# Another order of the attention work on ScalarE and VectorE

## What is computed

```python
xn = _layernorm(x, axis=-1)
q_latent, kv_latent = xn @ wq_down, xn @ wkv_down        # 192 and 64 wide
q = concat([q_latent @ wq_nope, rope(q_latent @ wq_rope)])
k = concat([kv_latent @ wk_nope, rope(kv_latent @ wk_rope)])
scores = einsum('bthd,bshd->bhts', q, k) / 192 ** 0.5     # causal mask
out = einsum('bhts,bshd->bthd', softmax(scores), kv_latent @ wv_up) @ wo
x = x + out + experts(xn)        # 32 experts, the best 8 of each token
```

## Time and profile before

| | before |
|---|---|
| median of 3 runs | 1176.25 us (1175.97 to 1178.59) |
| the profiled execution | 1180.77 us, its span 1179.0 us |
| TensorE busy | 1115.1 us, 95% of the span |
| VectorE busy | 723.4 us, 61% |
| ScalarE busy | 636.7 us, 54% |
| GpSimd busy | 493.7 us, 42% |

### The profile page before, as it was taken

How to read it: one execution, slowest core, us unless ns; L and a number is a source line. 1 busy time by engine, 2 the same in 40 slices (tenths; PEclk the granted TensorE clock), 3 DMA queues, 4 the chain that set the end, 5 groups by cost and what they waited for, 6 DMA issues and landing times. The chain is left out here.

```text
span 1179.0 us, 22440 instructions
## 1 busy us (share of the span) xinstructions
PE 1115.1 (95%) x7360; PEld 911.2 (77%) x7360; DVE 723.4 (61%) x1554; ACT 636.7 (54%) x1285; POOL 493.7 (42%) x386
## 2 busy tenths in 40 slices
PE   5859999999999999999999999899999999999997
PEld 3547778788788787787887887777888887888886
DVE  6657776676776776776776675545444445444444
ACT  3446666666666666666666666534343333334342
POOL 1083644643653653663653653222333332333332
PEclk9979999999999999999999999989999999999999
DMA  6101001001001001001000010065433333533332
GB/s 232 36 1 36 2 1 36 1 1 34 0 0 35 0 0 34 0 0 35 0 3 14 0 60 15 19 192 166 123 105 114 110 108 96 158 107 111 114 105 97
DMA packets 26309, 67.85 MB, mean 58 GB/s; under 512 B 3028, under 2 KB 9428, under 8 KB 26264
## 3 DMA queue, kind: packets, MB, share of 16 engines
q1 hardware_dynamic: 26120, 67.24, 18.8%
q10 hardware_dynamic: 144, 0.07, 0.0%
HBM read 62.82 MB, written 4.47 MB: 57 GB/s over the span
## 5 line engine op out<-in xcount | busy, mean ns | idle before, releaser
L736 ACT ACTIVATE prob<-ps_s,nm 128x128 f32<-128x128 f32 (+7 forms) x256 | 189.4, 740 | 209.0 <-DVE nm L896 208.1
L1339 POOL TENSOR_TENSOR hl<-hf,hh 128x512 fp32r<-128x512 f32 x96 | 123.6, 1287 | 295.4 <-ACT hh L1276 295.4
L896 DVE CUSTOM_DVE_ANT_0 ps_s<-ps_s,causal 128x128 f32<-128x128 f32 (+7 forms) x256 | 195.3, 765 | 54.4 <-PE ps_s L554 46.3
L565 PE MATMUL ps_t<-ident,prob 128*128 128x128 f32 x1152 | 177.2, 276 | 8.2 <-ACT pt L746 4.9
L565 PEld LDWEIGHTS ps_t<-ident,prob 128*128 128x128 f32 x1152 | 135.7, 141 | 36.1 <-issue 16.4
L577 PE MATMUL ps_o<-pt,kvn 128*64 128x128 f32 x2304 | 154.0, 278 | 0.5 <-DVE pt L905 0.4
L577 PEld LDWEIGHTS ps_o<-pt,kvn 128*64 128x64 f32 x2304 | 123.2, 136 | 33.3 <-issue 25.0
L905 DVE COPY pt<-ps_t 128x128 f32<-128x128 f32 (+2 forms) x192 | 102.1, 532 | 52.6 <-PE ps_t L565 52.2
L1308 DVE TENSOR_TENSOR gs<-gs,routing 128x512 f32<-128x512 f32 x64 | 44.3, 692 | 137.8 <-ACT gs L1272 137.8
L1276 ACT ACTIVATE hh<-hf 128x512 fp32r<-128x512 f32 x96 | 60.7, 633 | 121.6 <-DVE hf L1313 121.6
L1272 ACT ACTIVATE gs<-ps_g 128x512 f32<-128x512 f32 x96 | 57.4, 598 | 121.4 <-PE ps_g L1231 121.4
(11 more groups left out here) (271 smaller groups left out, 2571.4 us busy)
## 6 DMA issues: line engine op xcount, KB each, us to landing
routing<-wT_scratch SPq DMA_DIRECT2D x34, 256.0 KB, 3.7
raw_a<-in_e SPq DMA_DIRECT2D x17, 384.0 KB, 3.1
cosv<-in_e SPq DMA_DIRECT2D x17, 384.0 KB, 3.1
sinv<-wT_scratch SPq DMA_DIRECT2D x17, 384.0 KB, 3.6
raw<-in_e SPq DMA_DIRECT2D x17, 384.0 KB, 3.0
routing<-wT_scratch SPq DMA_DIRECT2D x16, 384.0 KB, 3.2
raw_a<-in_a SPq DMA_DIRECT2D x8, 512.0 KB, 3.3
raw_b<-in_b SPq DMA_DIRECT2D x8, 480.0 KB, 3.9
```

What stands on the lines that cost most here:

```text
L565: mm = nc.tensor.transpose(ps_t[x][:, at * P:(at + 1) * P], prob[t % 2][e][:, j * P:(j + 1) * P], ident[:, :])
L736: nc.scalar.activation(prob[t % 2][e][:, 0:len(halves) * width].rearrange("p (h k) -> p h k", k=width), ps_s[e][:, 0:len(halves), 0:width] ...
L896: nc.vector.tensor_tensor_reduce(out=s_ps, in0=s_ps, in1=bias, scale=-1.0, scalar=-MASKED, op0=ALU.add, op1=ALU.min, accum_out=nm[:, e:e + ...
L1339: nc.gpsimd.tensor_tensor(hl[:, c, :], hf[:, c, :], hh[:, c, :].bitcast(F32), ALU.subtract).then_inc(h_lo, 1)
```

## The change

Nothing is added or taken out; instructions of ScalarE and VectorE change places.

- ScalarE, tile 6: `latent_hi` of `QL1` now stands ahead of the first exponent, and `out_hi` behind the second `take_turned` (it stood ahead of the first exponent).
- ScalarE: `rope_hi` of `QR0` and of `KR0` stand at the end of tiles 3 and 4 (before: 4 and 5). `rope_hi` of `KR1` stands at the end of tile 0 (before: 1).
- VectorE, tile 2: `rope_products` of `KR0` stands behind the first maximum (before: ahead of it).
- VectorE, tile 3: `latent_low` of `QL0` stands behind the first maximum (before: ahead of it).

```diff
--- before.py
+++ after.py
@@ ScalarE, body(i), loop over the tiles t @@
-                        if t == TPC + 2:
-                            out_hi(s, 0, misc(i, b, "Yp1") if earlier else None)
+                        if more and t == TPC + 2:
+                            latent_hi(i, b, 1, 1 - b)
                         exponent(s, t, 0)
...
                         if more and t == 2:
                             latent_hi(i, b, 0, 1 - b)
-                        if more and t == TPC + 2:
-                            latent_hi(i, b, 1, 1 - b)
                         if has and (t == 0 or t > TPC):
                             take_turned(sp, tp, 1, 0)
+                        if t == TPC + 2:
+                            out_hi(s, 0, misc(i, b, "Yp1") if earlier else None)
                         exponent(s, t, 1)
                         if t == 0 and earlier:
                             widen(s - 1, 1)
-                        if more and t in (TPC, TPC + 1):
-                            rope_hi(s + 1, 0, 1 - b, (t - TPC,))
-                        if earlier and t == 1 and more:
+                        if more and t in (TPC - 1, TPC):
+                            rope_hi(s + 1, 0, 1 - b, (t - TPC + 1,))
+                        if earlier and t == 0 and more:
                             rope_hi(s, 1, b, (1,))
@@ VectorE, body(i), loop over the tiles t @@
                         if more and t == 1:
                             rope_products(i, b, "QR0", s + 1)
-                        if more and t == 2:
-                            rope_products(i, b, "KR0", s + 1)
-                        if more and t == 3:
-                            latent_low(i, b, 0, s + 1, 1 - b)
...
                         maximum(s, t, 0)
...
+                        if more and t == 2:
+                            rope_products(i, b, "KR0", s + 1)
                         if more and t == 3:
+                            latent_low(i, b, 0, s + 1, 1 - b)
                             rope_products(i, b, "QR1", s + 1)
```

## The result

The changed kernel took 1158.79 us, the median of 4 runs (1157.15 to 1159.53); the kernel before took 1176.20 (1175.97 to 1178.59). The ratio is 0.9845, with a 95% interval of 0.9828 to 0.9863: 1.5% faster. The forecast was 1153.5. So the time lies inside the stated range of 1151 to 1162, but 5.3 us above the forecast and 1.8 above the forecast's own range of 1151 to 1157: about a quarter of the expected 22.8 us is missing.

What follows compares the result with a forecast made beforehand. TensorE, busy 95% of the span, was taken as the bound, so only its waits counted: 8.0 + 6.0 + 6.8 + 1.1 + 0.9 = 22.8 us off 1176.25 gives 1153.5 us; own range 1151 to 1157, 8-in-10 range 1151 to 1162.

Steps and rivals of the forecast that it cites:

- A: In 14 of 16 stages tile 3's first scores wait for tile 2's first exponent; removing it gains 14 x 0.57 us.
- B: In six b = 0 stages the fold WA waits for `latent_low` of QL1; removing it gains 6 x 1.0 us.
- C: Between tiles 6 and 7 of b = 1 stages, turns wait for ScalarE's and VectorE's copies: 6 x 1.14 plus 1.1 us.
- D: A single TensorE wait at the start of the last stage; removing it gains 0.9 us.
- Covers at no cost: ScalarE's moved splits fit idle time before the exponents of tiles 1 and 4, so moving them costs zero.
- rival 2: The wait before tile 3's first scores moves to tile 5 in 14 stages: 8.0 us back, 1161.5 us; chance 0.10.
- Rival 3: Other waits end right behind the removed ones, so TensorE stands as long as before: 1176 us; chance 0.04.
- Rival 4: KR0's lows on GpSimd come too late for the next stage's first scores: slower, 1188 us; chance 0.06.
- The lock: VectorE instructions with two SBUF inputs and GpSimd instructions reading SBUF exclude each other; up to 0.78 us per blocked instruction.
- first rival: GpSimd blocks L881 or L883, delaying tile 7's maximum and exponent in 7 stages: 4.2 us back, 1157.7 us; chance 0.15.

Runs made afterwards that it cites:

- x5: The kernel before with VectorE's two moves alone (KR0's rotation, `latent_low` of QL0): 1176.63 us, ratio 0.9985 to 1.0004.
- x6: The kernel before with the `rope_hi` moves alone (QR0, KR0 and KR1): 1161.32 us, ratio 0.9835 to 0.9868.
- x9: The kernel before with only `rope_hi` of QR0 and KR0 moved, to the end of tiles 3 and 4: 1166.24 us (one run).
- x4: The kernel before with the tile-6 edit alone (`latent_hi` of QL1 and `out_hi` moved): 1167.26 us, ratio 0.9894 to 0.9927.
- x3: The changed kernel without its tile-6 edit (`latent_hi` of QL1 and `out_hi` as before): 1156.94 us, ratio 0.9803 to 0.9836.
- x2: The kernel before with L881 and L883 moved to the end of tile 4, while GpSimd makes its sums: 1188.47 us (one run).
- x1: The changed kernel with L881 and L883 moved ahead of the first maximum of tile 6, when GpSimd is idle: 1151.85 us.
- the repeat: The changed kernel measured again without any edit, beside other kernels on the same chip: 1157.14 us.
- x7: The changed kernel with `out_hi` of tile 6 put back ahead of the exponent and of QL1's splits: 1153.95 us, ratio 0.9791 to 0.9828.

## Why the prediction was right, and where it was not

**A, 14 x 0.57 = 8.0: right, with both its parts.** The exponent was late by KR1's splits, and the rotation of KR0 would have been the next to hold it, as the prediction worked out ("unmoved it would hold the exponent until 384.3"). x5 and x6 show one each: the first is the cause, the second the cause behind it. A place cost 0.61 and not 0.57; the earlier trace rows was a step with a score pass of another size.

**B, 6 x 1.0, and C, 6 x 1.14 + 1.1: the size right, the cause only half.** B was rounded down to 1.0 for nothing; it costs 1.14. C costs 1.13. But the prediction let them fall by two things at once, QL1's splits ahead of the exponent and an empty end of tile 5, and booked both under the tile-6 edit. Either is enough in the loop: x9 removes C and two thirds of B, x4 removes both. Only pair 0's C needs the tile-6 edit: x3 and x9 still have it, with printed waits of 0.52 and 0.49 us for ScalarE's copy and 0.19 for VectorE's (before 0.52 and 0.19). Two cures of one wait don't add: x4 gains 1.19 a loop, x3 3.18, together 4.37, and the change 2.85.

**D, 0.9: right.** No wait is printed at the start of the last stage.

**Covers at no cost: right.** The idle time ahead of tile 1's exponent fell from 1.96 to 0.80 us, and held KR1's 1.3; "some 0.6 left" was the forecast. Tile 5 didn't take over A (rival 2), but for the one place in pair 0, where 0.81 us of it stand. That stage lacks work of a stage before, and the prediction read its slack in a stage in the middle. Rival 3 is out, as the loop is 2.85 us shorter. Rival 4 is out: no wait for `keys` or `klo` came up at the start of a stage; x2, the one kernel that is slower than before, is so mainly by its waits for `yacc`.

**The lock: the step that failed.** The sum of the forecast put the lock at nothing, against its own first rival. That rival had the mechanism, the lines (L881, L883) and nearly the price: 4.2 us, where the loop and pair 0 give 6 x 0.71 + 0.45 = 4.7. It got a chance of 0.15 and came in all seven stages; the forecast, at 0.65, did not come. That the time is inside the stated range is due to this rival, which the range took in. Three of its steps fell short. First, whether the meeting happens was left as certain "in order, if not in time", and could have been worked out from rows of the kernel before:

```profile
362.13 2.63 POOL L1066 TENSOR_TENSOR klo<-t,khi 64x512 fp32r<-64x512 f32 x2 [0.22 <-ACT qhi L765]
366.51 0.35 DVE L881 CAST rhi<-raw_a 128x384 fp32r<-128x384 f32 x1
```

KR0's lows end at 364.76, and L881 starts 1.75 us later. By the prediction's own working the lows come 1.7 later, and `latent_low`, which stands ahead of `split_a` on VectorE, earlier. The two sides were moved towards each other until they met. Second, a blocked instruction cost more than 0.78: L881 1361 - 350 = 1.01 and L883 1526 - 558 = 0.97, together 1.98 against 1.6. Third, the reason against it, that the exponent of tile 7 is needed only in the next stage, looked at the exponent alone. What came late was the copy that stands behind it and QR1's two splits on ScalarE. So 1.98 us held up cost 0.71 by a path that the rival didn't have; that its price came so near is in part luck.

**The sum.** A pair of stages takes 2.85 us less, where 3.3 were forecast, and 3.56 less without the lock (x1). With the lock away (x1) the attention is 25.1 us shorter than before's, and the median 24.4: 22.8 was slightly too small. With it, 19.5 in the profiled executions. The medians say 17.4, and 19.1 for the repeat. The profile of before was 4.5 above its median; most of it is outside the attention, since it starts 1.7 us later there (70.84) and its end part is 2.3 us longer (409.9) than in most of the other kernels' profiles (69.03 to 69.4, and 407.6 to 408.6). So its waits can be taken for those of a median execution, as the prediction assumed.

The 2.1 us by which the medians' gain falls short of the 19.5 go with TensorE's granted clock. In after's profiled execution, which is at its median, the clock stands at 0.50 (1.2 GHz) from 745 to 751 us, where the attention ends and the mix begins, just behind a wait of TensorE of 2.23 us for `olo`; in the repeat's it stays at 1.00 (2.4 GHz) there. After's attention is 1.0 us longer than the repeat's and its mix 1.4 (409.15 against 407.7). Three of after's four runs had a mean clock of 0.988 and took 1158.66 to 1159.53 us; the fourth, at 0.993, took 1157.15. Before's profile has such a stretch as well (767 to 774 us), x1's has none, so of the 25.1 about 1 us is the clock's (an estimate: the 2 us from 767 to the mix at half speed). Why it falls in some executions and not in others stays open: the wait of 2.23 us is in all of these.

## What to carry to other kernels

When an order is changed, list for every instruction that moves, or whose producer moves, what an engine that can hold it up (here GpSimd for VectorE) does at its new time: work both times out from rows and don't leave them to chance. Follow a late instruction to the end of its in-order queue: what waits on it may be harmless, and what stands behind it not. Measure the edits of a reordering one by one; here one is worth 0 alone and 0.55 us a loop behind another, and two that cure the same wait are worth less than their two gains added.

## What was not expected of the hardware

- A cast with one input and one output in SBUF (L881, 128x384) was held up like the two-input subtraction: 350 to 1361 ns. It ended about 0.2 us after GpSimd's first instruction of `rope_low` (1.3 us each, from 355.41), and L883 behind it was held by the second. GpSimd's own times didn't show the meeting there (1.29 and 2.65 us, against 2.64 in the earlier trace rows); elsewhere they did, but less than VectorE's: the two lows behind x7's `out_low` took 2.94 us, and sums in x2 1.38 to 1.47 in place of 1.29.
- A wait may cost TensorE time and not be printed: 0.14 and 0.38 us from start to start in x6 and x3, and 0.29 in x4, with no idle time in brackets. Starts of the same instructions in two kernels show it; the list of waits doesn't.
